# Order of the hidden tiles split around group 0, its partial sums kept in SBUF, and a longer warm-up

## The chip, the core and the metric

The kernel runs on one core of a Trainium2 chip. The metric is the device time of one execution in microseconds (us). The core has TensorE (PE, matmuls; PEld are its weight loads), VectorE (DVE), ScalarE (ACT), GpSimd (POOL) and SyncE (SP), whose queue issues nearly all DMA transfers. SBUF is the working memory, PSUM holds what matmuls add up.

## What is computed

Input `x` has 32 batches of 64 rows of 512 numbers, so 2048 rows. A conditioning step makes `h0`, a feed-forward step follows, and `x` is added at the end:

```python
q_emb = relu(cond @ W3 + b3)                      # per batch
h0 = relu(((n * x + sum_over_n(x)) * q_emb) @ W2 + b2)   # n = 64
w1, w2 = ternary(W_fc), ternary(W_proj)           # groups of 64: sign * mean|w|, small ones 0
h = square(relu(h0 @ w1.T))                       # 2048 wide
hn = h * rsqrt(mean(h * h) + eps)
out = x + hn @ w2.T
```

The factor of the mean square belongs to a whole row, so the kernel applies it after the last product.

## The kernel before

**Groups, units and tiles.** The 2048 rows are four groups of 512. First come 16 units (4 per group): unit `u` makes a 128-row slice of `h0` for one group with 8 matmul instructions in full fp32 (`make_h0`, L291). Ahead of the third unit of group 0, 1 and 2 stands `sum_x` of the next group (L272, 32 matmul instructions), which needs that group's `x` in `x_sb` (`load_x`, L230). Then come 64 tiles: tile `v` is group `g = v // 16` and slice `j = v % 16` of the hidden layer. `hidden` (L307) makes it with 8 matmuls, ScalarE turns it into `relu_y`, `y` and `y_sq` (L555, L558, L561), VectorE splits `y` into `y_hi` and `y_lo` (`split_y`, L448 and L450), and `project` (L320) adds it into the four banks of `ps_out` with 8 matmuls, two tiles behind `hidden`. POOL adds up `y_sq` (L205, L209).

**Weights.** They come as 16 pairs of 128-row blocks, and each goes through a chain: SP loads it (`load_pair`, L215), ScalarE reads it twice (`read_pair`, L522 and L523), VectorE makes its scales (`sum_pair`, L408 and L411), ScalarE spreads them (`spread_pair`, L528), VectorE makes the ternary weights (`ternary_pair`, L418 to L424), SP turns them by a transposing DMA (`turn_pair`, L221), ScalarE keeps the result in `w_t` (`keep_pair`, L535). ScalarE's `step(i)` is `keep_pair(i - 2)`, `read_pair(i + 2)`, `spread_pair(i + 1)`, and VectorE's is `sum_pair(i + 1)`, `ternary_pair(i)`. The tables `STEP_AT_UNIT` and `STEP_AT_TILE` say behind which unit or tile a step stands in the orders of both engines.

**SP's queue.** It works strictly in order, and its loop over the pairs also holds the loads of the groups' `x`. `wt_ready` counts the `keep_pair` that are done, so `turn_pair(i)` follows `keep_pair(i - 1)`:

```python
def turn_pair(i):
    sp.wait_ge(tern_ready, i + 1)
    wait(sp, wt_ready, i)
    sp.dma_start_transpose(...)
for i in range(len(PAIRS)):
    load_pair(i + RAW_RING + 1); turn_pair(i)
    if i == 1: load_x(2)
    if i == 4: load_x(3)
```

**Ends of groups.** At the second tile of the next group (`v % 16 == 1`) VectorE does `inverse_root` and `finish` for the group that ended, ahead of `split_y(v)`: `finish` (L484) reads the four banks of `ps_out`, multiplies by `rstd`, adds `x_res` and writes `o_sb`. PE's first `project` of the next group waits for it bank by bank.

**Start.** PE waits for the constants of POOL and for `cond`, turns `cond` (L363), runs `WARM_UP` matmuls on the identity (L367), then the products with W3 (L372, "q" below) and `sum_x` of group 0 (L272).

Of the kernel before, what the change touches and what calls it, by code (L numbers as in the profile page):

```python
# [12 lines left out]
P = 128  # L13
# [12 lines left out]
WARM_UP = 6  # L26
# [7 lines left out]
def adaln_ffn(  # L34
# [12 lines left out]

    BATCHES, N, D = x.shape
# [11 lines left out]
    assert D == BANK and GROUPS == 4 and TT == 4 and KD == 4  # L60

# [25 lines left out]
    with ExitStack() as ctx:  # L87
# [45 lines left out]
        o_sb = x1_t[:, 0]  # L133
# [3 lines left out]
        sq_acc = wv_sb[:, SQ_RING, :]  # L137
# [5 lines left out]

        consts_ready = sem("consts_ready")
# [45 lines left out]
        finished = sem("finished")  # L190
        stored = sem("stored")
# [3 lines left out]
        def projected_at(v):  # L195

            g, j = v // HJ, v % HJ
            return (tile_summed, TT * (g + 1)) if j == HJ - 1 else (projected, (HJ - 1) * g + j + 1)

        def add_squares(engine, v):  # L200
            g, j = v // HJ, v % HJ
            engine.wait_ge(sq_ready, v + 1)
            if j == 1:
                wait(engine, part_summed, g)
                engine.tensor_tensor(sq_acc[:], y_sq[:, (v - 1) % SQ_RING, :], y_sq[:, v % SQ_RING, :], ALU.add  # L205
                                     ).then_inc(sq_added, 2)
# [63 lines left out]
        def _(pe):  # L270
# [24 lines left out]
            def hidden(v):  # L295
                g, j = v // HJ, v % HJ
# [29 lines left out]
            def project(v):  # L326
                g, j = v // HJ, v % HJ
                if g == 0 and j % TT == 0:
# [4 lines left out]
                if j < HJ - 1:  # L333
# [14 lines left out]
            def sum_squares(g):  # L348
                if g == GROUPS - 1:
                    pe.wait_ge(sq_added, HJ * (g + 1))  # L350
                    for t in range(TT):
                        last = pe.matmul(ps_sq[:, t:t + 1], sq_acc[:, t * P:(t + 1) * P], ones[:], start=True, stop=True)  # L352
# [4 lines left out]
                pe.wait_ge(part_summed, g + 1)  # L357
# [8 lines left out]
            for i in range(WARM_UP):  # L366
# [7 lines left out]
            last.then_inc(q_done, 1)  # L374
            for t in range(TT):
# [21 lines left out]
            sum_squares(GROUPS - 1)  # L397
# [3 lines left out]
        def _(dve):  # L401
# [253 lines left out]
```

## Time and profile before

| | before |
|---|---|
| time, median of 3 runs | 322.94 us (322.0 to 325.56) |
| profiled execution | 322.21 us, span 320.2 us |
| PE busy | 312.3 us, 98% of the span, 1324 instructions |
| VectorE, ScalarE, POOL busy | 66%, 60%, 35% |
| PE idle | first 4 us and last 4 us of the span, nearly nothing between |
| page's clock line | 9 (full) in all 40 slices |

A matmul's end is modelled, so a full PE row does not mean that matmuls start as fast as they could; their starts tell that. In rows of a timeline the columns are start, duration, engine, line, operation, output and inputs, sizes, how many in a row, and in brackets idle time of the engine just ahead. A group of matmuls that follow one another stands as one row.

### The profile page before, as it was taken

The page shows a single profiled execution, that of the slowest core. Times are in us where ns is not written, and L with a number is a line of the kernel's source. Part 1 is how long each engine was busy: PE and PEld are TensorE (multiplying, and loading weights), DVE is VectorE, ACT ScalarE, POOL GpSimd, SP SyncE. Part 2 cuts the span into 40 slices and gives each one's busy share as a digit, 9 for nine tenths or more (in the row PEclk, how much of TensorE's full clock was granted, in tenths as well). Part 3 has the DMA queues.
Part 4 walks back from the last instruction along what each step waited for, and adds up shares of the span by engine and source line. Part 5 has one row for each costly group of instructions (what it writes and reads, how often), then busy time and mean ns, then how long its engine had stood idle before and what let it go on. Part 6 is the DMA issues. An engine that isn't in the chain of part 4 may idle for free.

```text
span 320.2 us, 3832 instructions
## 1 busy us (share of the span) xinstructions
PE 312.3 (98%) x1324; PEld 237.8 (74%) x1324; DVE 210.4 (66%) x290; ACT 192.2 (60%) x282; POOL 113.1 (35%) x94
## 2 busy tenths in 40 slices
PE   5999999999999999999999999999999999999995
PEld 5764655544888788888888888888888888888884
DVE  0449989798898856677555665855665675665545
ACT  1659797899996885445554444654445554445550
POOL 1003333234643535414334441334443314443330
PEclk9999999999999999999999999999999999999999
DMA  6994959588411110007000000610000024000003
GB/s 199 299 311 114 282 130 271 142 189 248 119 36 34 33 36 1 0 14 250 0 0 2 0 0 0 215 51 0 0 2 0 0 105 159 0 0 2 0 1 132
DMA packets 31332, 27.02 MB, mean 84 GB/s; under 512 B 18737, under 2 KB 20817, under 8 KB 31313
## 3 DMA queue, kind: packets, MB, share of 16 engines
q1 hardware_dynamic: 29984, 26.25, 29.0%
q10 hardware_dynamic: 1328, 0.53, 0.7%
q8 instruction: 10, 0.16, 0.2%
q14 instruction: 10, 0.07, 0.1%
HBM read 18.39 MB, written 4.19 MB: 71 GB/s over the span
## 4 chain that ended last, share of the span: by engine, by line
PE 89%; ACT 4%; issue 3%; DVE 2%; DMA 1%; DVEq 0%; ACTq 0%
PE ps_out L320 34%; PE ps_acc L307 32%; PE ps_acc L291 17%; PE ps_out L272 4%; ACT x_t L558 1%; ACT x_t L555 1%; DMA h_f<-in_cond_dram 1%; PE ps_acc L367 1%; DVE abs_sum L408 1%; DVE y_hi L448 1%; PE ps_x L372 1%; ACT w_scale L528 0%; ACT w_t L535 0%; ACT w_abs L522 0%; PE ps_x L352 0%
## 5 line engine op out<-in xcount | busy, mean ns | idle before, releaser
L209 POOL TENSOR_TENSOR wv_sb<-wv_sb 128x512 f32<-128x512 f32 x55 | 82.2, 1495 | 114.0 <-ACT wv_sb L561 114.0
L320 PE MATMUL ps_out<-w_t,y_hi 128*128 128x512 f32 x256 | 101.7, 397 | 0.2 <-DVE y_lo L450 0.2
L320 PE MATMUL ps_out<-w_t,y_lo 128*128 128x512 f32 x256 | 101.0, 394 | 0.0
L307 PE MATMUL ps_acc<-h_hi,w_t 128*128 128x512 f32 x256 | 100.1, 391 | 0.0
L307 PE MATMUL ps_acc<-h_lo,w_t 128*128 128x512 f32 x256 | 100.0, 391 | 0.0
L450 DVE TENSOR_TENSOR y_lo<-x_t,y_hi 128x512 fp32r<-128x512 f32 x64 | 91.3, 1427 | 2.2
L555 ACT ACTIVATE x_t<-ps_acc 128x512 f32<-128x512 f32 x64 | 38.1, 595 | 81.1 <-PE ps_acc L307 81.0
L448 DVE CAST y_hi<-x_t 128x512 fp32r<-128x512 f32 x64 | 29.2, 457 | 73.5 <-PE ps_out L320 65.7
L320 PEld LDWEIGHTS ps_out<-w_t,y_hi 128*128 128x128 f32 x256 | 48.1, 188 | 11.6 <-DVE y_lo L450 0.6
L320 PEld LDWEIGHTS ps_out<-w_t,y_lo 128*128 128x128 f32 x256 | 48.3, 189 | 10.9
L307 PEld LDWEIGHTS ps_acc<-h_hi,w_t 128*128 128x128 f32 x256 | 48.3, 189 | 10.6 <-issue 0.2
L291 PE MATMUL ps_acc<-x_t,wv_sb 128*128 128x512 f32 x128 | 55.7, 593 | 0.3 <-DVE x_t L435 0.3
L307 PEld LDWEIGHTS ps_acc<-h_lo,w_t 128*128 128x128 f32 x256 | 48.1, 188 | 10.5 <-issue 0.2
L291 PEld LDWEIGHTS ps_acc<-x_t,wv_sb 128*128 128x128 f32 x128 | 24.0, 190 | 29.1 <-issue 28.7
L561 ACT ACTIVATE wv_sb<-x_t 128x512 f32<-128x512 f32 x64 | 40.5, 632 | 2.0
L558 ACT ACTIVATE x_t<-x_t 128x512 f32<-128x512 f32 x64 | 40.4, 631 | 2.0
L602 POOL TENSOR_TENSOR h_lo<-h_f,h_hi 128x512 fp32r<-128x512 f32 x16 | 20.4, 1274 | 60.1 <-DVE h_hi L442 60.1
L528 ACT ACTIVATE w_scale<-scale 128x1024 bf16<-128x1024 bf16 x16 | 16.8, 1048 | 5.6 <-DVE scale L411 5.6
L522 ACT ACTIVATE w_abs<-raw 128x1024 bf16<-128x1024 f32 x16 | 16.7, 1046 | 5.2 <-DMA raw<-in_L_ffn_W_proj_dram 3.8
L535 ACT ACTIVATE w_t<-w_turned 128x1024 fp32r<-128x1024 bf16 x16 | 16.8, 1050 | 5.1 <-DMA w_turned<-w_tern 5.1
L408 DVE TENSOR_REDUCE abs_sum<-w_abs 128x16 f32<-128x1024 bf16 x16 | 19.4, 1212 | 0.1
L523 ACT ACTIVATE w_sign<-raw 128x1024 bf16<-128x1024 f32 x16 | 16.7, 1043 | 0.0
(46 smaller groups left out, 144.0 us busy)
## 6 DMA issues: line engine op xcount, KB each, us to landing
x_sb<-in_x_dram SPq DMA_DIRECT2D x7, 1024.0 KB, 5.8
raw<-in_L_ffn_W_fc_dram SPq DMA_DIRECT2D x8, 512.0 KB, 5.9
raw<-in_L_ffn_W_proj_dram SPq DMA_DIRECT2D x8, 512.0 KB, 6.4
out_dram<-x_t SPq DMA_DIRECT2D x16, 256.0 KB, 2.1
x_sb<-in_x_dram SPq DMA_DIRECT2D x4, 256.0 KB, 5.6
wv_sb<-in_L_cond_W_dram SPq DMA_DIRECT2D x4, 256.0 KB, 7.0
x_t<-in_L_cond_W_dram ACTq DMA_DIRECT2D x1, 512.0 KB, 4.3
w_turned<-w_tern SPq DMA_TRANSPOSE x16, 3.1
```

The source lines that it names most:

```text
L209: engine.tensor_tensor(sq_acc[:], sq_acc[:], y_sq[:, v % SQ_RING, :], ALU.add).then_inc(sq_added, 1)
L291: last = pe.matmul(ps_acc[:, u % ACC_RING, :], wv_sb[:, k, m * P:(m + 1) * P], x1_t[:, g % RING, k, :], start=(k == 0), stop=(k == KD - 1))
L307: last = pe.matmul(ps_acc[:, (UNITS + v) % ACC_RING, :], w_t[:, j, k * P:(k + 1) * P], part[:, k, g * BANK:(g + 1) * BANK], start=(k == 0 ...
L320: last = pe.matmul(ps_out[:, t, :], part[:, v % RING, t * P:(t + 1) * P], w, start=(j == 0 and part is y_hi), stop=(j == HJ - 1 and part i ...
L408: dve.tensor_reduce(abs_sum[:], grouped(w_abs[:, i % READ_RING, :]), AX.X, ALU.add).then_inc(sum_ready, 1)
L448: dve.tensor_copy(y_hi[:, v % RING, :], y[:, v % RING, :]).then_inc(hi_done, 1)
L450: dve.tensor_tensor(y_lo[:, v % RING, :], y[:, v % RING, :], y_hi[:, v % RING, :], ALU.subtract).then_inc(split, 1)
L528: act.activation(w_scale[:, i % RING, :].rearrange("p (s w) -> p s w", w=TERN_GROUP), scale[:, i % RING, :].rearrange("p (s o) -> p s o", ...
L555: act.activation(relu_y[:, v % RING, :], ps_acc[:, (UNITS + v) % ACC_RING, :], ACT.Relu).then_inc(relued, 1)
L558: act.activation(y[:, v % RING, :], relu_y[:, v % RING, :], ACT.Square).then_inc(y_ready, 1)
L561: act.activation(y_sq[:, v % SQ_RING, :], y[:, v % RING, :], ACT.Square).then_inc(sq_ready, 1)
L602: pool.tensor_tensor(h0_lo[:, m, cols], h0_f[:, u % RING, :], h0_hi[:, m, cols], ALU.subtract).then_inc(h0_split, 1)
```

## The change

The tiles are taken in five stretches: tiles 0 to 7 are slices 0 to 7 of group 0, tiles 8 to 23 are group 1, tiles 24 to 31 are slices 8 to 15 of group 0, then groups 2 and 3. `START` is 0, 8, 24, 32, 48, 64. When the first stretch ends, `set_aside` copies the four banks to `partial` in SBUF; when the third ends, `merge` adds `ps_out` to `partial` and then makes the output from it. Outputs are written in place over `x_res`, so a load of the next `x_res` waits for the stores. `sq_acc` has two buffers. The weight steps are spread wider: step 0 to 10 in the units (0 to 11 before), 11 to 15 at tiles 1, 4, 7, 10, 13. At the start the identity is made first and has its own semaphore, 10 warm-up products stand ahead of the turn of `cond` and 2 behind it, and on ScalarE's queue the small `bq_t` goes ahead of W3 (`wq_sb`, which the trace calls `x_t`).

```diff
-WARM_UP = 6
+WARM_UP = 10
...
+    STRETCHES = [(0, 0, HJ // 2), (1, 0, HJ), (0, HJ // 2, HJ), (2, 0, HJ), (3, 0, HJ)]
+    TILE_AT = [(r, g, j) for r, (g, first, end) in enumerate(STRETCHES) for j in range(first, end)]
+    START = [sum(end - first for _, first, end in STRETCHES[:r]) for r in range(len(STRETCHES) + 1)]
+    def opens(v):
+        return v in START
+    def closes(v):
+        return v + 1 in START
...
-    STEP_AT_UNIT = {0: 0, 1: 1, 3: 2, 4: 3, 5: 4, 7: 5, 8: 6, 9: 7, 11: 8, 12: 9, 13: 10, 15: 11}
-    STEP_AT_TILE = {1: 12, 3: 13, 5: 14, 7: 15}
-    KEEP_AT_TILE = {8: 14, 9: 15}
+    STEP_AT_UNIT = {1: 0, 3: 1, 4: 2, 5: 3, 7: 4, 8: 5, 9: 6, 11: 7, 12: 8, 13: 9, 15: 10}
+    STEP_AT_TILE = {1: 11, 4: 12, 7: 13, 10: 14, 13: 15}
+    KEEP_AT_TILE = {15: 14, 16: 15}
...
-        o_sb = x1_t[:, 0]
+        partial = x1_t[:, 0]
...
-        sq_acc = wv_sb[:, SQ_RING, :]
+        sq_acc = wv_sb[:, SQ_RING:SQ_RING + 2, :]
...
-            def load_res(g):
-                if g == 0:
+            def load_res(n):
+                if n == 0:
                     sp.wait_ge(xt_done, KD * GROUPS)
                 else:
-                    sp.wait_ge(finished, TT * g)
-                sp.dma_start(x_res[:], x_rows[g]).then_inc(res_loaded, 16)
+                    sp.wait_ge(stored, 16 * TT * n)
+                sp.dma_start(x_res[:], x_rows[STRETCHES[n + 1][0]]).then_inc(res_loaded, 16)
...
-            for g in range(GROUPS):
+            for n in range(GROUPS):
                 for t in range(TT):
-                    sp.wait_ge(finished, TT * g + t + 1)
-                    sp.dma_start(out_rows[g, t], o_sb[:, t, :]).then_inc(stored, 16)
-                if g + 1 < GROUPS:
-                    load_res(g + 1)
+                    if n == 1:
+                        sp.wait_ge(merged, t + 1)
+                    else:
+                        sp.wait_ge(finished, TT * (n + 1) + t + 1)
+                    sp.dma_start(out_rows[STRETCHES[n + 1][0], t], x_res[:, t, :]).then_inc(stored, 16)
+                if n + 1 < GROUPS:
+                    load_res(n + 1)
...
-                if g == 0 and j % 2 == 0:
+                if v < 2 * HJ and g == j // (HJ // 2) and j % 2 == 0:
                     pe.wait_ge(wt_ready, ready_pairs(j))
-                if j == 0:
+                if opens(v):
                     pe.wait_ge(h0_split, KD * (g + 1))
...
-            pe.wait_ge(consts_ready, 1)
+            pe.wait_ge(ident_ready, 1)
+            for i in range(WARM_UP):
+                pe.matmul(ps_acc[:, 1, 0:P], ident_f[:], ident_f[:], start=True, stop=True)
             pe.wait_ge(cond_loaded, 16)
             for k in range(KQ):
                 last = pe.transpose(ps_acc[:, 0, k * BATCHES:(k + 1) * BATCHES], cond_sb[:, k * P:(k + 1) * P],
                                     ident_f[0:BATCHES, 0:BATCHES])
             last.then_inc(condt_done, 1)
-            for i in range(WARM_UP):
+            for i in range(2):
...
+            pe.wait_ge(consts_ready, 1)
...
+            def set_aside():
                 for t in range(TT):
-                    dve.wait_ge(tile_summed, TT * g + t + 1)
-                    dve.scalar_tensor_tensor(out=o_sb[:, t, :], in0=ps_out[:, t, :], scalar=rstd[:, t:t + 1],
+                    dve.wait_ge(tile_summed, t + 1)
+                    dve.tensor_copy(partial[:, t, :], ps_out[:, t, :]).then_inc(finished, 1)
+            def merge(r):
+                inverse_root(r)
+                for t in range(TT):
+                    dve.wait_ge(finished, t + 1)
+                    dve.wait_ge(tile_summed, TT * r + t + 1)
+                    dve.tensor_tensor(partial[:, t, :], ps_out[:, t, :], partial[:, t, :], ALU.add).then_inc(finished, 1)
+                dve.wait_ge(rstd_ready, r)
+                dve.wait_ge(res_loaded, 16 * r)
+                dve.wait_ge(finished, TT * (r + 1))
+                for t in range(TT):
+                    dve.scalar_tensor_tensor(out=x_res[:, t, :], in0=partial[:, t, :], scalar=rstd[:, t:t + 1],
+                                             in1=x_res[:, t, :], op0=ALU.mult, op1=ALU.add).then_inc(merged, 1)
+            def finish(r):
+                inverse_root(r)
+                dve.wait_ge(rstd_ready, r)
+                dve.wait_ge(res_loaded, 16 * r)
+                for t in range(TT):
+                    dve.wait_ge(tile_summed, TT * r + t + 1)
+                    dve.scalar_tensor_tensor(out=x_res[:, t, :], in0=ps_out[:, t, :], scalar=rstd[:, t:t + 1],
                                              in1=x_res[:, t, :], op0=ALU.mult, op1=ALU.add).then_inc(finished, 1)
+            def read_out(r):
+                if r == 0:
+                    set_aside()
+                elif STRETCHES[r][0] == 0:
+                    merge(r)
+                else:
+                    finish(r)
...
-                    inverse_root(v // HJ - 1)
-                    finish(v // HJ - 1)
+                r = TILE_AT[v][0]
+                if r > 0 and v == START[r] + AHEAD - 1:
+                    read_out(r - 1)
...
+            act.dma_start(bq_t[:], b_q.rearrange("(m p) -> p m", p=P), allow_slow_non_contiguous=True).then_inc(bias_loaded, 16)
             act.dma_start(wq_sb[:], w_q.rearrange("(k p) d -> p k d", p=P)).then_inc(wq_loaded, 16)
-            act.dma_start(bq_t[:], b_q.rearrange("(m p) -> p m", p=P), allow_slow_non_contiguous=True).then_inc(bias_loaded, 16)
...
+            pool.memset(ident_f[:], 0.0).then_inc(cleared, 1)
+            pool.wait_ge(cleared, 1)
+            pool.affine_select(out=ident_f[:], in_=ident_f[:], compare_op=ALU.not_equal, fill=1.0, base=0,
+                               pattern=[[-1, P]], channel_multiplier=1).then_inc(ident_ready, 1)
```

**ScalarE, units 1 to 4.** The first place is ScalarE's order at the second weight steps. `h_f<-ps_acc` is the reading of a unit (`relu_h0`), `w_t<-w_turned` is `keep_pair`, `w_abs` and `w_sign` are `read_pair`, `w_scale` is `spread_pair`. Before, from the reading of unit 0 on:

```order
L550 ACTIVATE h_f<-ps_acc,bv_t 128x512
L522 ACTIVATE w_abs<-raw 128x1024
L523 ACTIVATE w_sign<-raw 128x1024
L528 ACTIVATE w_scale<-scale 128x1024
L550 ACTIVATE h_f<-ps_acc,bv_t 128x512 x2
L535 ACTIVATE w_t<-w_turned 128x1024
```

With the change, from the same reading on:

```order
L606 ACTIVATE h_f<-ps_acc,bv_t 128x512
L578 ACTIVATE w_abs<-raw 128x1024
L579 ACTIVATE w_sign<-raw 128x1024
L584 ACTIVATE w_scale<-scale 128x1024
L606 ACTIVATE h_f<-ps_acc,bv_t 128x512 x2
L578 ACTIVATE w_abs<-raw 128x1024
L579 ACTIVATE w_sign<-raw 128x1024
L584 ACTIVATE w_scale<-scale 128x1024
L606 ACTIVATE h_f<-ps_acc,bv_t 128x512
L591 ACTIVATE w_t<-w_turned 128x1024
```

The first `keep_pair` stood behind three readings of units and now stands behind four, and one whole read and spread has moved ahead of it.

**SP, the second load of `x`.** The second place is SP's queue, where nothing moved; `raw` are weight loads, `x_sb` is `load_x(2)`:

```order
L239 DMA_TRANSPOSE w_turned<-w_tern 128x8x128 [waits tern_ready]
L233 DMA raw<-in_L_ffn_W_fc_dram 128x2x512 [waits sign_ready]
L239 DMA_TRANSPOSE w_turned<-w_tern 128x8x128 [waits wt_ready,tern_ready]
L248 DMA x_sb<-in_x_dram 128x4x512 [waits xt_done]
L233 DMA raw<-in_L_ffn_W_proj_dram 128x2x512 [waits sign_ready]
```

The load of `x` stands behind a transpose that waits for `wt_ready`, in both kernels.

**VectorE, the end of a stretch.** The third place is VectorE's order at the end of a group before:

```order
L475 SCALAR_TENSOR_TENSOR rstd<-h_f 128x4 [waits newton]
L484 SCALAR_TENSOR_TENSOR x_t<-ps_out,rstd,x_sb 128x512 [waits tile_summed,res_loaded,rstd_ready]
L484 SCALAR_TENSOR_TENSOR x_t<-ps_out,rstd,x_sb 128x512 [waits tile_summed] x3
L448 CAST y_hi<-x_t 128x512 [waits tile_summed,y_ready]
L450 TENSOR_TENSOR y_lo<-x_t,y_hi 128x512 [waits hi_done]
```

and with the change at tile 33, where the second half of group 0 ends (the first `x_t` here is `partial`):

```order
L504 SCALAR_TENSOR_TENSOR rstd<-h_f 128x4 [waits newton]
L519 TENSOR_TENSOR x_t<-ps_out,x_t 128x512 [waits tile_summed,finished] x4
L524 SCALAR_TENSOR_TENSOR x_sb<-x_t,rstd,x_sb 128x512 [waits finished,res_loaded,rstd_ready]
L524 SCALAR_TENSOR_TENSOR x_sb<-x_t,rstd,x_sb 128x512 x3
L476 CAST y_hi<-x_t 128x512 [waits tile_summed,y_ready]
L478 TENSOR_TENSOR y_lo<-x_t,y_hi 128x512 [waits hi_done]
```

Four instructions of 128x512 stand between `rstd` and the next split before, and eight with the change.

## Rows read from the trace of the kernel before

**Rows 1.** The waits: engine, line waited for, us in total, times, longest.

```profile
PEld ps_out L272 <- DMA x_sb<-in_x_dram: 0.2, 1, 0.2
...
PE ps_out L320 <- DVE y_lo L450: 0.2, 1, 0.2
```

**Rows 2.** The timeline of PE from 28 to 60 us.

```profile
37.29 3.73 PE L272 MATMUL ps_out<-sum_mat,x_sb 128*128 128x128 f32 x32
40.86 13.90 PE L291 MATMUL ps_acc<-x_t,wv_sb 128*128 128x512 f32 x32
54.59 3.73 PE L272 MATMUL ps_out<-sum_mat,x_sb 128*128 128x128 f32 x32
```

**Rows 3.** The DMA issues by line: count, KB each, median us to landing.

```profile
x_sb<-in_x_dram SPq DMA_DIRECT2D x7, 1024.0 KB, 5.8
...
x_t<-in_L_cond_W_dram ACTq DMA_DIRECT2D x1, 512.0 KB, 4.3
w_turned<-w_tern SPq DMA_TRANSPOSE x16, 3.1
...
bv_t<-in_L_cond_b_dram ACTq DMA_DIRECT2D x1, 2.0 KB, 6.4
```

**Rows 4.** The timeline of SP's queue around `load_x(2)` and `load_x(3)`.

```profile
29.59 1.24 SPq L221 DMA_TRANSPOSE w_turned<-w_tern  x1
30.87 0.58 SPq L230 DMA_DIRECT2D x_sb<-in_x_dram  x1
...
47.48 0.58 SPq L230 DMA_DIRECT2D x_sb<-in_x_dram  x1
```

**Rows 5.** The timelines of ScalarE and VectorE in units 2 and 3.

```profile
27.31 1.25 ACT L550 ACTIVATE h_f<-ps_acc,bv_t 128x512 f32<-128x512 f32 x2
28.45 1.05 ACT L535 ACTIVATE w_t<-w_turned 128x1024 fp32r<-128x1024 bf16 x1
29.39 1.05 ACT L522 ACTIVATE w_abs<-raw 128x1024 bf16<-128x1024 f32 x1
...
27.66 0.69 DVE L424 TENSOR_TENSOR w_tern<-w_abs,w_scale 128x1024 bf16<-128x1024 bf16 x1
```

**Rows 6.** The timeline of the first 14 us, all engines.

```profile
0.74 0.44 ACTq L567 DMA_DIRECT2D x_t<-in_L_cond_W_dram  x1
0.74 0.20 POOL L604 MEMSET sum_mat<- 128x128 f32 x1 [0.29 <-POOLq L643]
...
1.73 0.53 ACTq L569 DMA_DIRECT2D bv_t<-in_L_cond_b_dram  x1
1.77 0.29 POOL L611 TENSOR_SCALAR_AFFINE_SELECT sum_mat<-sum_mat 128x128 f32<-128x128 f32 x1 [0.24 <-POOL sum_mat L609]
...
4.18 2.93 PE L367 MATMUL ps_acc<-ident_f 128*128 128x128 f32 x12
...
6.91 2.20 PE L372 MATMUL ps_x<-h_f,x_t 128*128 128x32 f32 x16
...
8.94 3.82 PE L272 MATMUL ps_out<-sum_mat,x_sb 128*128 128x128 f32 x32
...
13.04 7.10 PE L291 MATMUL ps_acc<-x_t,wv_sb 128*128 128x512 f32 x16 [0.28 <-DVE x_t L435]
```

**Rows 7.** The timeline at the end of group 0, VectorE, POOL and PE.

```profile
142.14 2.73 DVE L484 SCALAR_TENSOR_TENSOR x_t<-ps_out,rstd,x_sb 128x512 f32<-128x512 f32 x4
...
143.91 0.40 PE L320 MATMUL ps_out<-w_t,y_hi 128*128 128x512 f32 x1
...
145.23 0.69 DVE L450 TENSOR_TENSOR y_lo<-x_t,y_hi 128x512 fp32r<-128x512 f32 x1
...
146.11 1.50 POOL L209 TENSOR_TENSOR wv_sb<-wv_sb 128x512 f32<-128x512 f32 x1 [1.58 <-ACT wv_sb L561]
...
146.50 1.66 DVE L450 TENSOR_TENSOR y_lo<-x_t,y_hi 128x512 fp32r<-128x512 f32 x1
...
147.59 0.40 PE L320 MATMUL ps_out<-w_t,y_hi 128*128 128x512 f32 x1
```

More of the change, by code:

```diff
@@ L312, in project_tile @@
             def project_tile(v, t):
-                g, j = v // HJ, v % HJ
+                r, g, j = TILE_AT[v]
                 c, i = j // TT, j % TT
                 w = w_t[:, HJ + KD * c:HJ + KD * (c + 1), i * P:(i + 1) * P]
-                if j == 0:
-                    wait(pe, finished, TT * (g - 1) + t + 1)
+                if opens(v):
+                    wait(pe, finished, TT * (r - 1) + t + 1)
                 for part in (y_hi, y_lo):
                     last = pe.matmul(ps_out[:, t, :], part[:, v % RING, t * P:(t + 1) * P], w,
-                                     start=(j == 0 and part is y_hi), stop=(j == HJ - 1 and part is y_lo))
-                if j == HJ - 1:
+                                     start=(opens(v) and part is y_hi), stop=(closes(v) and part is y_lo))
+                if closes(v):
                     last.then_inc(tile_summed, 1)
@@ L326, in project @@
             def project(v):
-                g, j = v // HJ, v % HJ
-                if g == 0 and j % TT == 0:
+                r, g, j = TILE_AT[v]
+                if v < 2 * HJ and g == j // (HJ // 2) and j % TT == 0:
                     pe.wait_ge(wt_ready, ready_pairs(HJ + KD * (j // TT) + 2))
@@ L332, in project @@
                     last = project_tile(v, t)
-                if j < HJ - 1:
+                if not closes(v):
                     last.then_inc(projected, 1)
@@ L346, in project_last_two, with sum_squares @@
                     project_tile(TILES - 1, t)
-            def sum_squares(g):
-                if g == GROUPS - 1:
-                    pe.wait_ge(sq_added, HJ * (g + 1))
+            def sum_squares(r):
+                if r == GROUPS:
+                    acc = sq_acc[:, STRETCHES[r][0] % 2, :]
+                    pe.wait_ge(sq_added, START[r + 1])
                     for t in range(TT):
-                        last = pe.matmul(ps_sq[:, t:t + 1], sq_acc[:, t * P:(t + 1) * P], ones[:], start=True, stop=True)
+                        last = pe.matmul(ps_sq[:, t:t + 1], acc[:, t * P:(t + 1) * P], ones[:], start=True, stop=True)
                     last.then_inc(sq_summed, 1)
@@ L389, in _ @@
                 hidden(v + AHEAD)
-                if v % HJ == HJ - 1:
-                    sum_squares(v // HJ)
+                r = TILE_AT[v][0]
+                if closes(v) and r > 0:
+                    sum_squares(r)
                 project(v)
@@ L450, in split_y, with sum_parts, inverse_root @@
                 dve.tensor_tensor(y_lo[:, v % RING, :], y[:, v % RING, :], y_hi[:, v % RING, :], ALU.subtract).then_inc(split, 1)
-            def sum_parts(g):
-                dve.wait_ge(sq_added, HJ * (g + 1))
-                wait(dve, sq_summed, g)
-                dve.tensor_reduce(part_sq[:], sq_acc.rearrange("p (j b) -> p j b", b=QUAD), AX.X, ALU.add,
+            def sum_parts(r):
+                acc = sq_acc[:, STRETCHES[r][0] % 2, :]
+                dve.wait_ge(sq_added, START[r + 1])
+                wait(dve, sq_summed, r - 1)
+                dve.tensor_reduce(part_sq[:], acc.rearrange("p (j b) -> p j b", b=QUAD), AX.X, ALU.add,
                                   apply_transpose=True).then_inc(part_summed, 1)
-            def inverse_root(g):
-                dve.wait_ge(sq_summed, g + 1)
-                if g == GROUPS - 1:
+            def inverse_root(r):
+                dve.wait_ge(sq_summed, r)
+                if r == GROUPS:
                     dve.tensor_scalar(mean_sq[:], ps_sq[:, 0:TT], 1.0 / H, RMS_EPS, ALU.mult, ALU.add).then_inc(mean_ready, P // QUAD)
-                for q in range(P // QUAD if g < GROUPS - 1 else 0):
+                for q in range(P // QUAD if r < GROUPS else 0):
                     rows = slice(q * QUAD, (q + 1) * QUAD)
@@ L503, in _ @@
             for v in range(TILES):
-                if v % HJ == AHEAD - 1 and v >= HJ:
-                    inverse_root(v // HJ - 1)
-                    finish(v // HJ - 1)
+                r = TILE_AT[v][0]
+                if r > 0 and v == START[r] + AHEAD - 1:
+                    read_out(r - 1)
                 if v == TILES - 2:
@@ L509, in _ @@
                 split_y(v)
-                if v % HJ == HJ - 1 and v < TILES - 1:
-                    sum_parts(v // HJ)
+                if closes(v) and 0 < r < GROUPS:
+                    sum_parts(r)
                 if v in STEP_AT_TILE:
                     step(STEP_AT_TILE[v])
-            inverse_root(GROUPS - 1)
-            finish(GROUPS - 1)
+            read_out(GROUPS)
         @block.scalar
@@ L586, in _ @@
             for v in range(TILES):
-                if v % HJ == AHEAD - 1 and v >= HJ:
-                    take_root(v // HJ - 1)
+                r = TILE_AT[v][0]
+                if r > 1 and v == START[r] + AHEAD - 1:
+                    take_root(r - 1)
                 hidden_tile(v)
```

49 lines of the change are left out of this document (22 added, 27 removed).

## The prediction

> **What bounds the kernel now.** I read the busy times first: PE is busy 98% of the span, so whatever makes PE wait is time. Then PE's waits and the starts in its timeline. Between its first long product at 13.04 us [rows 6] and the last 4 us of the span, the only wait of a matmul that the view lists is 0.2 us for `y_lo`, once; the loads of weights list 0.2 us for `x_sb` [rows 1]. A unit takes (54.59 - 40.86) / 4 = 3.43 us and `sum_x` 40.86 - 37.29 = 3.57 us [rows 2], a tile 147.59 - 143.91 = 3.68 us also where a group ends [rows 7]. None of that arithmetic is removed. So the change can win only at the start, at that one 0.2 us, and loses wherever it makes PE wait. What matters is how much slack each releaser of PE has, and one has nearly none: the load of `x` for group 2 is issued at 30.87 [rows 4], a load of `x` lands 5.8 us after its issue [rows 3], so at 36.7, and PE starts on it at 37.29 [rows 2]. The 0.2 us of waiting on `x_sb` says the same.
>
> **Later weight steps, second load of x: +2.1 us.** SP issues `load_x(2)` behind `turn_pair(1)`, and that one waits for the first `keep_pair`. Before, `keep_pair(0)` runs at 28.45 for 1.05 us [rows 5] and the transpose is issued at 29.59, the load 1.28 us later [rows 4]. The steps now stand later: step 1 behind unit 2's reading, step 2 behind unit 3's. I follow ScalarE by PE's pace. Unit 2 ends at 37.29 - 3 x 3.43 = 27.0. Its reading takes 0.62 (half of 1.25) and ends at 27.7. Step 1 has no keep; its two reads take 0.94 each (28.45 to 29.39 is the spacing of such instructions [rows 5]) and its spread 0.95, so ScalarE is free at 30.6. Unit 3 ends at 30.4, its reading at 31.2, `keep_pair(0)` at 31.2 + 1.05 = 32.25. VectorE is no later: the third product of its step 1 ended at 27.66 + 0.69 = 28.35 in unit 1 [rows 5]; now the step starts behind the reading of unit 2, at 28.1, and takes about 3.6 (28.1 to 31.7). So the transpose goes at 32.35, the load of `x` at 33.6, and it lands at 39.4. PE wants it at 37.29: it waits 2.1 us. With a landing in 5.5 us and quick handovers it would be 1.7, with 6.2 us 2.5.
>
> **Third load of x: +3.0 us.** `load_x(3)` stands behind `turn_pair(4)`, which needs `keep_pair(3)`, in step 5. Step 5 stood at unit 7 and now stands at unit 8, and step 4 at unit 7 right ahead of it. PE, with the first wait: `sum_x` ends at 39.4 + 3.6 = 43.0, unit 6 at 46.4, unit 7 at 49.9, unit 9 at 56.7, where it wants `x`. ScalarE: the reading of unit 6 ends at 47.1, `keep_pair(2)` at 48.1, the rest of step 4 at 50.9, the reading of unit 7 at 51.5. `turn_pair(3)`, issued at 48.2 behind `keep_pair(2)`, lands 3.1 us later [rows 3], at 51.3, so it holds nothing up. `keep_pair(3)` ends at 52.55, the transpose goes at 52.6, the load at 53.9 (47.48 before [rows 4]) and lands at 59.7. PE waits 3.0 us; between 2.2, if ScalarE gets by with less, and 3.6, if the weight load ahead of it on the same queue slows it. Later units and all of `load_res` have no such deadline.
>
> **Weights in the tiles: -0.2 us.** Second-half weights are now needed at tile 16 on, not at 8, and the steps come every third tile. A step costs VectorE about 3.6 us and ScalarE 3.8; over two tiles (7.4 us) with two splits that was just too much, over three (11.0) it isn't. The wait of 0.2 us for `y_lo` [rows 1] goes.
>
> **`set_aside`: 0.** Four copies out of PSUM, at the price of `finish`, 2.73 for four [rows 7], without an inverse root ahead of them. PE computes a whole `hidden` tile (half of 3.68) before it needs the first bank, and needs the others half a microsecond apart. They start behind tile 8's split and end over 2 us before tile 9's project wants its split. If step 13 in front of them held VectorE long enough to use that cover up, PE would wait up to 1 us.
>
> **`merge`: +2.45 us.** This is the other edit on the path. Before, `finish` runs from 142.14 to 144.87, the next split ends at 145.23 + 0.69 = 145.92, and PE's `project` on it starts at 147.59 [rows 7]: slack 1.67 us. With the change the four adds take the place of `finish` (one input in PSUM as there, 2.73) and release the banks in time. Behind them, and ahead of the split, come four more instructions over 128x512, with both tensors in SBUF. Below: 0.69 each as `y_lo` alone, 2.76, so the split ends 1.1 us late. But POOL adds squares in that stretch: the row at 146.11, 1.50 long. The split at 146.50 stands beside it and takes 1.66 instead of 0.69: it ends 0.55 us after POOL, so it had stood still [rows 7], while `finish` with its PSUM input keeps 0.68 each. Where POOL's 146.11 falls the third of the four would start; it waits some 1.3 us. Sum: 2.76 + 1.3 + handover 0.1 - 1.67 = 2.5, taken as 2.45. Behind the split in VectorE's queue is only the next split, with slack, so it is paid once.
>
> The Trainium skill has the rule on this (SBUF — State Buffer, Who interferes with whom): a VectorE instruction with two SBUF inputs and a GpSimd one that reads SBUF exclude each other for the whole instruction, one with a single SBUF input doesn't contend. The trace agrees for `y_lo` (1.66 against 0.69); for this form of instruction no row of before shows it. By the rule the merge costs 2.45, without it 1.1 to 1.2.
>
> **Start: -0.4 us.** POOL clears and selects the identity first: 0.74 + 0.20 + 0.24 + 0.29 = 1.5 us [rows 6], so 20 warm-up instructions (two per product) run while `cond` and W3 still travel. Before, 12 of them take 6.91 - 4.18 = 2.73 us, 0.228 each; 32 of the same size in `sum_x` take 3.57, 0.112 each [rows 2, 6]. The first are at the lower of the clock's two levels by that ratio, though the page's clock line says full. 20 at the slow pace end at 5.9 to 6.1; the turn of `cond` and the copy behind it take some 0.7. So q starts at 6.7, near the 6.91 of before, and gains mostly from the clock: 16 x 0.112 = 1.8 against 8.94 - 6.91 = 2.03 [rows 6]. Sum 0.4. Best case: fast clock from 5 us on, q at 5.9, gain 1.1. Against it stands W3: it landed 4.3 us after its issue as the first of the queue [rows 3]; now it comes behind `bq_t`, so at 5.5 at the earliest and at 1.73 + 6.4 = 8.1, where the last of the three landed, at the latest. At 8.1 the start would lose about 1.
>
> **Sum.** 2.1 + 3.0 - 0.2 + 2.45 - 0.4 = +6.95 us. The profiled execution had 322.21 us, so 329.2; the median of the runs is 0.7 higher, which the range has to hold.
>
> **Rivals.**
> *Loads on time, chance 0.13.* If keeps and handovers let SP issue `load_x(2)` by 37.29 - 5.8 = 31.5, PE doesn't wait there; with both loads on time only the merge stays: 322.2 + 2.45 - 0.6 = 324.1. This is the case that isn't slower by what can be told, and would be less still (321.6) if the merge had cover as well. For it: the loads may land faster in a less crowded queue. Against it: the order fixes three ScalarE instructions and a unit ahead of the keep, and 31.5 lies 2.1 us before my 33.6.
> *Merge hidden or half price, chance 0.13.* Without POOL's part or with faster instructions: 326.8 to 328.0, still slower.
> *The clock falls while PE waits, chance 0.1.* Two idle stretches of 2 to 3 us in a row are new. At the slow pace `sum_x` takes 32 x 0.228 = 7.3 instead of 3.6, so each wait could cost 3.7 more: 333 to 337. No row of before has such a wait past the start, so neither is shown. The Trainium skill (TensorE: Matmul & The Clock Gate, Why this matters for your kernels) warns that idle stretches between bursts of matmuls bring the slow clock back.
> *Faster, chance 0.02.* The start's best case, 1.1, with the loads on time and the merge covered, gives 321.0 or 0.6% under the median; for over 1% the start would have to beat that bound by 1.3 us.
> *My forecast, 0.62.* 329.2, own range 326.5 to 331.
>
> **How the numbers follow.** Three runs of before spread by 1%, so about 1% is what a measurement can tell from no change. Slower by over 1% (above 326.2): the forecast, the clock and the merge rival, 0.62 + 0.1 + 0.13 = 0.85. Same: the loads-on-time case, 0.13. Faster 0.02. The range reaches from 325.5 (both loads at their lower bounds, start at its best, merge at 1.2: 322.2 + 1.7 + 2.2 + 1.2 - 1.3 = 326.0, and a bit of the next case) to 332.0 (upper bounds 2.5 + 3.6 + 2.6 and no gain at the start, 330.9, and the offset of the median).
>
> **What would show it.** PE's waits list `sum_x` twice for the `x_sb` DMA, 2 and 3 us; SP's timeline has the loads of `x` at 33 to 34 and near 54. At tile 33 PE waits for `y_lo` over 2 us, and two of the four merging instructions are 0.69 long, one over 1.5. W3's products start before 7 us. If `x_sb` isn't among PE's waits, the main step is wrong; if all four merging instructions are 0.69 the lock is.

## The result, and the profile after

The changed kernel takes 334.9 us (median of 4, 333.92 to 336.15) against 323.6 us for the kernel before (median of 4): the ratio is 1.0358, with a 95% interval of 1.0303 to 1.0413. The forecast of 329.2 us had the sign right and was 5.7 us short, and the time lies above its range.

First the page of the changed kernel: its busy times, and of the slices the lines of PE and of its clock.

```profile
span 334.2 us, 3866 instructions
...
PE 318.9 (95%) x1336; PEld 243.7 (73%) x1336; DVE 216.3 (65%) x298; ACT 192.1 (57%) x282; POOL 113.0 (34%) x94
...
PE   8999699399999999999999999979999999999995
...
PEclk9999899789999999999999999999999999999999
```

PE's share fell from 98% to 95%. There are three dents in its line, two in the units and one two thirds of the way along, and behind the first two stands a lower clock. The waits of the changed kernel name them (engine, line waited for, total, times, longest):

```profile
PEld ps_out L294 <- DMA x_sb<-in_x_dram: 9.7, 2, 6.1
...
PE ps_out L294 <- DMA x_sb<-in_x_dram: 8.0, 2, 5.3
...
PE ps_out L342 <- DVE y_lo L478: 1.9, 1, 1.9
```

The timeline of PE in the units, in the changed kernel, answers to [rows 2, 6]:

```profile
1.52 4.24 PE L386 MATMUL ps_acc<-ident_f 128*128 128x128 f32 x20 [1.52 <-POOL ident_f L663]
...
6.49 1.87 PE L398 MATMUL ps_x<-h_f,x_t 128*128 128x32 f32 x16
...
12.29 7.11 PE L313 MATMUL ps_acc<-x_t,wv_sb 128*128 128x512 f32 x16 [0.28 <-DVE x_t L463]
...
22.80 13.90 PE L313 MATMUL ps_acc<-x_t,wv_sb 128*128 128x512 f32 x32
39.38 5.44 PE L294 MATMUL ps_out<-sum_mat,x_sb 128*128 128x128 f32 x32 [2.68 <-DMA x_sb<-in_x_dram]
44.65 13.90 PE L313 MATMUL ps_acc<-x_t,wv_sb 128*128 128x512 f32 x32
63.87 6.78 PE L294 MATMUL ps_out<-sum_mat,x_sb 128*128 128x128 f32 x32 [5.32 <-DMA x_sb<-in_x_dram]
70.49 20.77 PE L313 MATMUL ps_acc<-x_t,wv_sb 128*128 128x512 f32 x48
...
220.51 0.50 PE L342 MATMUL ps_out<-w_t,y_hi 128*128 128x512 f32 x1 [1.89 <-DVE y_lo L478]
```

By starts, four units still take 13.73 us. So the second `sum_x` was due at 22.80 + 13.73 = 36.53 and began at 39.38, 2.85 late; the third was due at 58.38 and began at 63.87, 5.49 late. They also run longer: 44.65 - 39.38 = 5.27 and 70.49 - 63.87 = 6.62 us, against 3.57 in [rows 2], so 1.70 and 3.05 more. The last row is the third dent, at tile 33: PE's product ahead of it began at 218.23 and the next was due 0.23 us later, at 218.46, so by starts it is 2.05 late. The windows of the changed kernel, one on each of the two and one between, have the granted clock (columns: us of the window, busy of PE, PEld, DVE, ACT, POOL, granted clock, DMA share, GB/s):

```profile
39.30:42.80 3.50, 3.42 (x16) 3.42 (x17) 1.15 (x3) 0.50 (x1) 1.26 (x1) 0.51 1.03 283
42.80:45.00 2.20, 2.20 (x19) 2.05 (x19) 1.53 (x3) 0.00 (x0) 0.00 (x0) 1.00 0.00 0
...
63.30:70.00 6.70, 6.13 (x28) 6.13 (x29) 2.42 (x4) 0.43 (x1) 1.26 (x1) 0.50 0.63 148
```

A granted 0.5 is the level of 1.2 GHz instead of 2.4. The full account of the span: start -0.75 (12.29 against 13.04), waits +2.85 and +5.49, slow clock +1.70 and +3.05, the third dent +2.05, the wait at tile 6 of before -0.35 (there `project` began at 106.70 instead of 106.35), together 14.04 us, and 334.2 - 320.2 is 14.0.

### The profile page after: what moved, and what is told of

Its sections match the earlier page's. It is cut to its first block, busy times and chain, and to the rows that moved or that the text cites. A ratio compares the mean times of both kernels' runs of the same rounds, so it can differ in the third digit from the quotient of the medians.

```text
span 334.2 us, 3866 instructions
## 1 busy us (share of the span) xinstructions
PE 318.9 (95%) x1336; PEld 243.7 (73%) x1336; DVE 216.3 (65%) x298; ACT 192.1 (57%) x282; POOL 113.0 (34%) x94
## 4 chain that ended last, share of the span: by engine, by line
PE 83%; DMA 6%; DVE 4%; ACT 2%; issue 2%; SPq 1%; POOL 0%; DVEq 0%; POOLq 0%; ACTq 0%
PE ps_out L342 35%; PE ps_acc L329 34%; PE ps_acc L313 7%; PE ps_out L294 5%; DMA x_sb<-in_x_dram 4%; DMA raw<-in_L_ffn_W_proj_dram 2%; PE ps_acc L386 1%; DVE x_sb L524 1%; DVE abs_sum L436 1%; ACT w_scale L584 1%; ACT w_t L591 1%; DVE x_t L519 1%; DVE x_t L463 1%; ACT h_f L606 1%; PE ps_x L398 1%
## 5 line engine op out<-in xcount | busy, mean ns | idle before, releaser
L478 DVE TENSOR_TENSOR y_lo<-x_t,y_hi 128x512 fp32r<-128x512 f32 x64 | 90.3, 1410 | 2.2
L476 DVE CAST y_hi<-x_t 128x512 fp32r<-128x512 f32 x64 | 30.6, 478 | 67.6 <-PE ps_out L342 63.9
L294 PE MATMUL ps_out<-sum_mat,x_sb 128*128 128x128 f32 x128 | 19.8, 327 | 8.0 <-DMA x_sb<-in_x_dram 8.0
L294 PEld LDWEIGHTS ps_out<-sum_mat,x_sb 128*128 128x128 f32 x128 | 19.2, 241 | 10.1 <-DMA x_sb<-in_x_dram 9.7
L606 ACT ACTIVATE h_f<-ps_acc,bv_t 128x512 f32<-128x512 f32 x16 | 10.8, 675 | 20.5 <-PE ps_acc L313 20.5
L470 DVE CAST h_hi<-h_f 128x512 fp32r<-128x512 f32 x16 | 7.8, 487 | 18.4 <-ACT h_f L606 18.4
```

Source lines behind the costliest of these rows:

```text
L294: return pe.matmul(ps_out[:, k, t * P:(t + 1) * P], x_sb[:, t, k * P:(k + 1) * P], sum_mat[:], start=True, stop=True)
L476: dve.tensor_copy(y_hi[:, v % RING, :], y[:, v % RING, :]).then_inc(hi_done, 1)
L478: dve.tensor_tensor(y_lo[:, v % RING, :], y[:, v % RING, :], y_hi[:, v % RING, :], ALU.subtract).then_inc(split, 1)
```

## The experiments

Each change to an edit is given against the changed kernel or the kernel before, as said. The spans stand beside 320.2 us before and 334.2 us after.

**Both loads of `x` early.** Against the changed kernel:

```diff
             for i in range(len(PAIRS)):
...
-                if i == 1:
+                if i == 0:
                     load_x(2)
-                if i == 4:
+                if i == 2:
                     load_x(3)
```

> The changed kernel with the loads of x for groups 2 and 3 taken out from behind the transposes that wait for a keep: load_x(2) behind turn_pair(0), load_x(3) behind turn_pair(2). Theory A (SP's order makes both loads late, and TensorE's clock falls because TensorE idles for them): no wait of sum_x on x_sb, granted clock 1.00 to the end, both sum_x at 3.57 us; the span loses 2.85 + 1.70 + 5.49 + 3.05 = 13.1 us of 334.2 and comes to 321.1, the time to about 323. Rival B (the clock falls for another reason, such as the long warm-up or the new start, and only the waits are SP's): the waits go, sum_x stays at 5.3 and 6.6 us, span about 325.9. Rival C (the loads land late because the queues are fuller): waits of 1 us or more stay.

Measured: span 321.4 us, time 323.7 us (10 runs), ratio to before 0.9991 (0.9954 to 1.0028). PE's timeline in this kernel:

```profile
36.91 3.73 PE L294 MATMUL ps_out<-sum_mat,x_sb 128*128 128x128 f32 x32
40.48 13.90 PE L313 MATMUL ps_acc<-x_t,wv_sb 128*128 128x512 f32 x32
54.22 3.73 PE L294 MATMUL ps_out<-sum_mat,x_sb 128*128 128x128 f32 x32
57.79 20.77 PE L313 MATMUL ps_acc<-x_t,wv_sb 128*128 128x512 f32 x48
```

No bracket is left and both `sum_x` take 3.57. Two lines of SP's order carry 12.8 of the 14.0 us. The start and its long warm-up stand unchanged here, and the granted clock of the profiled execution is 1.00 in all stretches up to the last product, so they were not what lowered it.

**The second load alone.** As above, with `load_x(3)` left behind `turn_pair(4)`.

> The changed kernel with load_x(2) alone behind turn_pair(0), load_x(3) where the change has it. Theory A1 (the third load is late by itself, for keep_pair(3) stands behind two steps in a row and a transpose that lands late): no wait at the second sum_x, a wait of about 5 us and a slow third sum_x remain, span 321.1 + 5.2 + 3.0 = 329.3. Rival A2 (most of the third wait follows from the first wait and the slow clock behind it): the third wait is under 3 us, the clock stays full or nearly, span 321 to 325.

Measured: span 329.0 us, one execution. PE's timeline in this kernel:

```profile
40.51 13.90 PE L313 MATMUL ps_acc<-x_t,wv_sb 128*128 128x512 f32 x32
59.08 6.22 PE L294 MATMUL ps_out<-sum_mat,x_sb 128*128 128x128 f32 x32 [4.67 <-DMA x_sb<-in_x_dram]
65.13 20.77 PE L313 MATMUL ps_acc<-x_t,wv_sb 128*128 128x512 f32 x48
```

The third `sum_x` is late by 59.08 - (40.51 + 13.73) = 4.84 us and takes 6.05. The third load is late by itself. It isn't a consequence of the first wait.

**The step tables alone, on the kernel before.**

```diff
-    STEP_AT_UNIT = {0: 0, 1: 1, 3: 2, 4: 3, 5: 4, 7: 5, 8: 6, 9: 7, 11: 8, 12: 9, 13: 10, 15: 11}
-    STEP_AT_TILE = {1: 12, 3: 13, 5: 14, 7: 15}
-    KEEP_AT_TILE = {8: 14, 9: 15}
+    STEP_AT_UNIT = {1: 0, 3: 1, 4: 2, 5: 3, 7: 4, 8: 5, 9: 6, 11: 7, 12: 8, 13: 9, 15: 10}
+    STEP_AT_TILE = {1: 11, 3: 12, 5: 13, 7: 14, 9: 15}
+    KEEP_AT_TILE = {10: 14, 11: 15}
```

> The kernel before, with nothing changed but the step tables: units as in the change, tiles 1, 3, 5, 7, 9 and the last two keeps at tiles 10 and 11. Theory A: the table alone makes both loads late: waits of about 2.5 to 3.5 and 5 to 5.5 us for x_sb, two slow sum_x, span 320.2 + 13 = 333, plus up to 0.5 in the tiles, where a fifth step now stands. Rival D (the waits need the new order at the start or of the tiles as well): span under 325.

Measured: four executions took 336.03, 334.03, 336.63 and 328.57 us, with a mean granted clock of 0.984, 0.990, 0.984 and 1.000. The profiled one (span 334.0 us) has both waits in PE's timeline:

```profile
42.34 5.47 PE L272 MATMUL ps_out<-sum_mat,x_sb 128*128 128x128 f32 x32 [2.62 <-DMA x_sb<-in_x_dram]
47.64 13.90 PE L291 MATMUL ps_acc<-x_t,wv_sb 128*128 128x512 f32 x32
64.67 6.71 PE L272 MATMUL ps_out<-sum_mat,x_sb 128*128 128x128 f32 x32 [3.13 <-DMA x_sb<-in_x_dram]
```

So the table by itself makes both loads late, with no new order of tiles and no new start: by starts the waits are 2.79 and 3.30 us, and the two `sum_x` take 5.30 and 6.54. Part of this profiled execution's time lies elsewhere: its first long product begins at 15.30 instead of 13.04, with the clock still low in the products ahead of it, and PE waits some 1.0 us for `y_lo` in the tiles, where a step stands at every second tile to the end. The fourth execution, with a mean clock of 1.000, took 328.57 us, which is still above all 13 executions of the kernel before that stand beside it (321.42 to 326.14). The other three took 5.5 to 8.1 us more; in the profiled one the two slow `sum_x` make 1.73 + 2.97 us, and it starts 2.26 us later than the profile of the kernel before. How the fourth one spent its time isn't known, as it has no trace.

**Work for PE while it waits.** Against the changed kernel, the loads as late as ever:

```diff
+FILL = {1: 0, 2: 11, 3: 22}
...
             def sum_x(g):
+                for i in range(FILL[g]):
+                    pe.matmul(ps_x[:, 0:P], ident_f[:], ident_f[:], start=True, stop=True)
                 pe.wait_ge(x_loaded, 16 * g)
```

> The changed kernel with products on the identity (11 and 22, as at the start, into ps_x) ahead of the second and third waits for x, so that TensorE works while it waits and the loads stay as late. Theory A: the clock stays full, both sum_x take 3.57 us; the span loses 1.70 + 3.05 = 4.75 us and comes to about 329.4, the loads land as late as before. Rival B (the clock falls for another reason than TensorE's idling): sum_x stays slow, span 334 or more.

Measured: span 329.8 us; three executions took 331.48 to 332.0 us. A fourth took 467.07 us with a mean granted clock of 0.656; it is left out, and what happened in it stays open, as it wasn't profiled. Against the kernel before the ratio is 1.0224 (1.0152 to 1.0297). PE's timeline, and below it two windows on the two `sum_x`:

```profile
37.64 2.62 PE L300 MATMUL ps_x<-ident_f 128*128 128x128 f32 x22
40.12 3.84 PE L295 MATMUL ps_out<-sum_mat,x_sb 128*128 128x128 f32 x32
43.79 13.90 PE L316 MATMUL ps_acc<-x_t,wv_sb 128*128 128x512 f32 x32
57.52 5.08 PE L300 MATMUL ps_x<-ident_f 128*128 128x128 f32 x44
62.44 3.74 PE L295 MATMUL ps_out<-sum_mat,x_sb 128*128 128x128 f32 x32
```

```profile
40.10:43.80 3.70, 3.70 (x35) 3.69 (x34) 2.52 (x5) 0.47 (x1) 1.27 (x1) 1.00 0.98 244
...
62.40:66.00 3.60, 3.60 (x34) 3.60 (x34) 2.07 (x3) 0.00 (x0) 0.60 (x1) 1.00 0.42 144
```

Products that nobody needs keep the clock at 1.00 and `sum_x` at 3.67 and 3.57 us, and the kernel gets faster by 4.4 us in span although the start of this execution was 1.1 us later (13.39 against 12.29). This shows that the clock fell because PE idled. The loads were also somewhat less late here: `sum_x` began 40.12 - 37.64 = 2.48 and 62.44 - 57.52 = 4.92 us after it was due, instead of 2.85 and 5.49. So 4.65 of the 5.6 us won in the two stretches are the pace of `sum_x`, and 0.94 are shorter waits.

**The start alone, on the kernel before.**

```diff
-WARM_UP = 6
+WARM_UP = 10
...
-            pe.wait_ge(consts_ready, 1)
+            pe.wait_ge(ident_ready, 1)
+            for i in range(WARM_UP):
+                pe.matmul(ps_acc[:, 1, 0:P], ident_f[:], ident_f[:], start=True, stop=True)
             pe.wait_ge(cond_loaded, 16)
...
-            for i in range(WARM_UP):
+            for i in range(2):
...
+            act.dma_start(bq_t[:], b_q.rearrange("(m p) -> p m", p=P), allow_slow_non_contiguous=True).then_inc(bias_loaded, 16)
             act.dma_start(wq_sb[:], w_q.rearrange("(k p) d -> p k d", p=P)).then_inc(wq_loaded, 16)
-            act.dma_start(bq_t[:], b_q.rearrange("(m p) -> p m", p=P), allow_slow_non_contiguous=True).then_inc(bias_loaded, 16)
```

> The kernel before, with nothing changed but the start: identity first, 10 warm-up products ahead of the turn of cond and 2 behind, bq_t ahead of W3. Theory A (the start brings what the trace of the change shows): first long product near 12.3 to 12.7 us instead of 13.04, the rest as before, span 319.5 to 319.9, the time 0.5 to 1.5 us under the kernel before, since warm-up at full clock comes earlier in more of the executions. Rival E (the longer warm-up brings nothing in time, W3 or the loads bound the start): 320.2, within 0.3 us of before.

Measured: 322.83 us (12 runs), ratio 0.9973 (0.9940 to 1.0007), span of the profiled execution 321.2 us. The time can't be told from no change by this interval. Its timelines of PE, ScalarE and SP show why this execution won nothing:

```profile
23.52 14.24 PE L292 MATMUL ps_acc<-x_t,wv_sb 128*128 128x512 f32 x32
38.13 3.84 PE L273 MATMUL ps_out<-sum_mat,x_sb 128*128 128x128 f32 x32 [0.36 <-DMA x_sb<-in_x_dram]
...
22.16 1.06 ACT L526 ACTIVATE w_abs<-raw 128x1024 bf16<-128x1024 f32 x1 [5.08 <-DMA raw<-in_L_ffn_W_proj_dram]
...
32.09 0.58 SPq L231 DMA_DIRECT2D x_sb<-in_x_dram  x1
```

The start itself brought nothing here: the first long product begins at 13.01, against 13.04 before. The second `sum_x`, due at 23.52 + 13.73 = 37.25, begins at 38.13, not because PE came earlier, but because the load of `x` was issued at 32.09 instead of 30.87. Ahead of it in the chain ScalarE's read of a pair waited for the weight load until 22.16; in the kernel before it began at 20.94. So the load's slack of half a microsecond goes as soon as a weight load lands 1.2 us later. Whether the new start made it land later, or chance, isn't shown.

**The split ahead of the merged output.** Against the kernel with both loads early:

```diff
             def merge(r):
...
-                dve.wait_ge(rstd_ready, r)
+
+            def merge_out(r):
+                dve.wait_ge(rstd_ready, r)
...
                 split_y(v)
+                if r == 3 and v == START[3] + AHEAD - 1:
+                    merge_out(2)
```

> The changed kernel with the loads of x early (as in e1_loads_early) and the four instructions that write the merged output moved behind the split of tile 33. Theory A (the wait of 2.05 us at tile 33 is the four instructions ahead of the split): the wait goes, span 321.4 - 2.05 = 319.35. Rival F (the adds or the root ahead of them make that wait): 1 us or more of it stays, span above 320.4.

Measured: span 319.3 us, 321.26 us (12 runs, 320.54 to 321.80), ratio 0.9932 (0.9901 to 0.9963). The only waits of PE in it:

```profile
PE ps_acc L386 <- POOL ident_f L667: 1.5, 1, 1.5
PE ps_acc L313 <- DVE x_t L463: 0.3, 1, 0.3
```

The four instructions take 3.76 us as before, but nobody waits for them. This version beats both kernels, the one before by 0.7%. It also spreads less than the kernel with the loads early, which had runs from 322.97 to 325.75 us, four of its ten at a mean clock of 0.995, all of those above 325; here all twelve are at 1.000 and lie within 1.3 us.

**POOL held back at the merge.** Against the kernel with both loads early, first until the merged output is written, then until the split behind it is done as well:

```diff
             for v in range(TILES - 1):
+                if v == START[3] + AHEAD:
+                    pool.wait_ge(merged, TT)
```

```diff
             for v in range(TILES - 1):
+                if v == START[3] + AHEAD:
+                    pool.wait_ge(split, START[3] + AHEAD)
```

> The changed kernel with the loads of x early (as in e1_loads_early), and POOL's add of the squares of tile 34 held back until the merged output is written. Theory A (VectorE stands still for POOL's add while it writes the merged output): the four instructions take 2.8 instead of 3.77 us and TensorE waits 1.0 to 1.1 instead of 2.05 us at tile 33, span 320.4. Rival G (instructions with both tensors in SBUF take that long by themselves): they stay at 3.7 us, the wait at 2.05, span 321.4.

> As e7_pool_later, but POOL's add of the squares of tile 34 is held back until tile 33 is split as well, since in e7_pool_later it ran beside that split's y_lo (1.63 instead of 0.69 us) and gave the gain back there. Theory A (exclusive use of SBUF by VectorE's two-tensor instructions and POOL): the four instructions take 2.74, y_lo 0.69, TensorE waits 1.0 to 1.1 instead of 2.0 us at tile 33, span 320.4. Rival G: another wait takes its place and the span stays at 321.4.

Measured: span 321.4 us for the first, 320.6 for the second. The rows of VectorE and POOL at tile 33, first with the loads early alone, then with POOL behind the output, then with POOL behind the split:

```profile
202.91 3.77 DVE L524 SCALAR_TENSOR_TENSOR x_sb<-x_t,rstd,x_sb 128x512 f32<-128x512 f32 x4
...
207.06 0.69 DVE L478 TENSOR_TENSOR y_lo<-x_t,y_hi 128x512 fp32r<-128x512 f32 x1
...
204.28 1.86 POOL L227 TENSOR_TENSOR wv_sb<-wv_sb 128x512 f32<-128x512 f32 x1 [1.58 <-ACT wv_sb L617]
```

```profile
202.94 2.74 DVE L524 SCALAR_TENSOR_TENSOR x_sb<-x_t,rstd,x_sb 128x512 f32<-128x512 f32 x4
...
206.05 1.63 DVE L478 TENSOR_TENSOR y_lo<-x_t,y_hi 128x512 fp32r<-128x512 f32 x1
...
205.76 1.38 POOL L227 TENSOR_TENSOR wv_sb<-wv_sb 128x512 f32<-128x512 f32 x1 [3.03 <-DVE x_sb L524]
```

```profile
202.93 2.74 DVE L524 SCALAR_TENSOR_TENSOR x_sb<-x_t,rstd,x_sb 128x512 f32<-128x512 f32 x4
...
206.04 0.69 DVE L478 TENSOR_TENSOR y_lo<-x_t,y_hi 128x512 fp32r<-128x512 f32 x1
```

Without POOL beside them the four take 2.74 instead of 3.77 us. In the first of the two the gain was given back one instruction later, since POOL's add now met `y_lo`; my expectation had missed that. With both clear, PE waits 0.9 us at tile 33 instead of 1.9. The remaining 0.9 fits the four instructions themselves, 2.74 us against the 1.67 us of slack in the kernel before.

**The order of tiles, by leaving it out.** The kernel before with the start of the change and both loads early.

> The kernel before with the start of the change (as e5_start_alone) and both loads of x early, its order of tiles and its step tables as before. It tells what the order of tiles itself is worth against e6_split_first. Theory A: the wait of 0.88 us for x that the earlier start brought in e5_start_alone goes, the wait for y_lo at tile 6 stays (0.3), span 319.3 + 0.3 = 319.6 to 320.0, within 0.3% of e6_split_first. Rival H (the order of tiles is what makes e6_split_first fast): 321 or more.

Measured: 324.43 us (12 runs), ratio 0.9996 (0.9965 to 1.0027), span 322.8 us. I had expected a span of 319.6 to 320.0. PE waits in this kernel, and a row of ScalarE:

```profile
PE ps_out L321 <- DVE y_lo L454: 1.1, 1, 1.1
PE ps_acc L308 <- ACT h_f L554: 0.7, 1, 0.7
...
50.20 1.06 ACT L539 ACTIVATE w_t<-w_turned 128x1024 fp32r<-128x1024 bf16 x1 [4.78 <-DMA w_turned<-w_tern]
```

The waits are at the first tiles, where units and weight steps end. ScalarE comes there late, and its row shows where it lost the time: the transpose issued at 42.31, right behind the third load of `x` (41.29) and a weight load (41.70), landed 7.9 us later, and ScalarE stood still for it for 4.78 us. With twelve steps to fit into the units instead of eleven it had little idle time behind that, 1.18 us in one place, and didn't catch up. With the change's tables the third load goes at 40.68 in the kernel with the loads early, and the next transpose only at 45.83, 4.9 us to landing; PE waits for nothing there. So the measured time is on the side of rival H, but what the traces show at work is the place of the steps, which the tables set and for which the new order of tiles makes room; the order by itself wasn't tested. In the profiled executions the spans differ by 3.5 us, of which 0.5 is the start (13.18 against 12.68) and most of the rest these two waits. The medians differ by 324.43 - 321.26 = 3.2 us, by the ratios to the kernel before only 0.64%, or 2.1 us, as they were taken beside slower executions of it. How much of it is the table and how much the order wasn't taken apart.

## Why the prediction was wrong, and where it was right

**What bounds the kernel: right.** PE's waits are the whole account, and the load of `x` with nearly no slack was the one that broke.

**Later steps, second load: right.** The forecast had the load issued at 33.6 and landed at 39.4. SP's timeline of the changed kernel:

```profile
32.12 1.24 SPq L239 DMA_TRANSPOSE w_turned<-w_tern  x1
33.40 0.58 SPq L248 DMA_DIRECT2D x_sb<-in_x_dram  x1
...
50.00 1.24 SPq L239 DMA_TRANSPOSE w_turned<-w_tern  x1
...
57.32 0.58 SPq L248 DMA_DIRECT2D x_sb<-in_x_dram  x1
```

The load went at 33.40, and `sum_x` began at 39.38. The wait was 2.85 instead of 2.1 because PE arrived 0.75 us earlier than before, from the better start, while the load went only 0.2 us earlier than forecast. ScalarE had its reading of unit 2 earlier too, but its spread then waited 0.43 us for VectorE's `scale`, a wait that the forecast didn't have. So the two terms weren't independent, and the early start in front of a late load was worth nearly nothing.

**Third load: mechanism right, size wrong.** 3.0 was forecast, with 3.6 as the upper bound, and 5.49 measured. Two durations were taken from medians of the rows. The transpose issued at 50.00 held `keep_pair(3)` up until 54.91:

```profile
54.91 1.06 ACT L591 ACTIVATE w_t<-w_turned 128x1024 fp32r<-128x1024 bf16 x1 [1.57 <-DMA w_turned<-w_tern]
```

That is 4.9 us, not 3.1, and ScalarE stood still for 1.57 us of it; the load of `x` took from 57.32 to about 63.8, so 6.5 and not 5.8. The two make 2.3 of the 2.5 us that the term was short. Over the kernels here transposes landed in 3.1 to 7.9 us. Where this one landed in 3.1 (the table-only kernel), the wait was 3.3 us by starts, close to the forecast. What makes one land late stays open.

**The clock: the step that failed.** The sum took PE's waits at their length alone and put the clock behind them at nothing. The prediction had it as a rival at 0.1, with 3.7 us per wait and 333 to 337 in all, and set the range's upper end without it. All four executions of the changed kernel have a mean granted clock of 0.983 to 0.990, so it happened in each, and it costs 1.70 + 3.05 = 4.75 us in the profile. The price per wait was right as a bound; the chance was the error. That 334.9 lies in the rival's 333 to 337 is in part luck: the rival added up to 7.4 us of clock to waits of 5.1, and the trace has 4.75 of clock behind waits of 8.34. I gave it 0.1 because no row of before had an idle PE past the start, which was an absence of evidence, not evidence. By the rule of the Trainium skill (TensorE: Matmul & The Clock Gate, Why this matters for your kernels), idle stretches between bursts bring the slow clock back; the trace agrees (granted clock 0.51 behind the wait of 2.85 us, 0.50 behind that of 5.49). Taking the sum without the clock and with the measured waits, 322.2 - 0.75 + 2.85 + 5.49 - 0.35 + 2.05 = 331.5, would have been within the range; the forecast with the clock's 4.75 and nothing else mended, 333.9, would not. So the clock alone takes the time out of the range, and the short third term alone does not.

**Weights in the tiles and `set_aside`: right.** PE has no wait at tile 6 nor at tile 8; the four copies took 2.48 us.

**`merge`: right.** 2.45 was forecast and 2.05 measured. The adds take 2.48 instead of 2.73, the four writing instructions 3.77 instead of 4.06, with POOL's add among them: three of them are 0.75 long and one 1.78. The rule of the Trainium skill cited there (SBUF — State Buffer, Who interferes with whom) holds for this form of instruction too: 2.74 alone, 3.77 with POOL's add.

**Start: not settled.** -0.4 was forecast and -0.75 found in the profiled execution of the changed kernel, but that was the best of nine: with this start the first long product begins at 12.29 to 13.39 us, 12.8 on average, against 13.04 in the one profile before and 15.30 in the table-only kernel, whose start is the same as before. Over many executions the start alone gives 0.27% at the best estimate, and its interval reaches no change.

## What to carry to other kernels

When a table of steps is moved, follow what a strictly ordered queue holds behind the moved work, its transfers for other stages above all: here two loads of `x` stood behind transposes that waited for a step of ScalarE, and taking them out gave 12.8 of 14.0 us back. A wait of TensorE can have a second price, since the engine may come out of it at half the clock: so it did here behind each of the five traced waits of 2.8 to 5.5 us that it idled through, and behind none of the traced ones of some 2 us at tile 33. Count it in the sum, not in a rival. Work put ahead of an instruction that an engine's neighbour waits for should be asked whether it can stand behind it: moving four instructions one place back took a wait of 2 us out.

## What was not expected of the hardware

What a wait costs in clock doesn't seem to be the same in every execution of one program: with the table alone on the kernel before, three executions at a mean granted clock of 0.984 to 0.990 took 334.0 to 336.6 us and one at 1.000 took 328.57. Perhaps even the wait of 2.05 us at tile 33 is enough in some executions: in the kernel with the loads early, four of ten runs have a mean clock of 0.995 and are about 2 us longer, and none with that wait gone. These runs have no trace of their own, so where in them the clock fell was not seen; in the profiled one it stays at 1.00 behind that wait. Two things speak for caution. By its mean the lower clock accounts for 1.0 to 1.6 of the 2 us, if half of the time at half clock is lost (estimated from 0.995 against 0.998 and 1.000, over 323 us). And the kernel before, which has no such wait, spreads over 321.3 to 326.4 us with means of 0.997 to 1.000, so most of its spread isn't in that mean at all.

A mean a little under 1.000 need not cost anything either. In the profiled execution with the loads early, at 0.998, the only low stretch that the profile shows lies in the last 1.4 us of the span, behind the last product (columns as in the windows above):

```profile
320.00:321.00 1.00, 0.00 (x0) 0.00 (x0) 0.00 (x0) 0.00 (x0) 0.00 (x0) 0.51 0.25 94
```

The clock's release at the start also moves: of the 16 products with W3, all run at the fast pace in the changed kernel (1.87 us, against 2.20 before), while in the profiled execution of the table-only kernel they take 3.46 and the `sum_x` behind them 5.16 instead of 3.82 us, though the program ahead of them is that of the kernel before.
